# Causal mask added by VectorE on its way out of the banks, and two instructions moved in linear attention, in a six-layer decoder kernel

## The reference, cut to what matters

```python
def _L0_attn_ref(x, ...):                       # 16 heads of 16 features
    ...
    q = jnp.concatenate([q_c, _apply_rope(q_e, cos, sin)], axis=-1)
    k = jnp.concatenate([k_c, _apply_rope(k_e, cos, sin)], axis=-1)
    scores = jnp.einsum('bhqd,bhkd->bhqk', q, k) * scale
    causal = jnp.tril(jnp.ones((t, t), dtype=bool))
    scores = jnp.where(causal[None, None], scores, -jnp.inf)
    att = jax.nn.softmax(scores, axis=-1)
    y = jnp.einsum('bhqk,bhkd->bhqd', att, v)
    y = y.transpose(0, 2, 1, 3).reshape(b, t, c)
    return y @ Wc

def _L1_attn_ref(x, Wq, bq, Wk, bk, Wv, bv, Wo, bo):   # linear attention, 16 heads
    ...
    sink_incoming = 1.0 / jnp.einsum('nhld,nhd->nhl', q + EPS, k.sum(axis=2) + EPS)
    source_outgoing = 1.0 / jnp.einsum('nhld,nhd->nhl', k + EPS, q.sum(axis=2) + EPS)
    conserved_sink = jnp.einsum('nhld,nhd->nhl', q + EPS, (k * source_outgoing[..., None]).sum(axis=2) + EPS)
    conserved_source = jnp.einsum('nhld,nhd->nhl', k + EPS, (q * sink_incoming[..., None]).sum(axis=2) + EPS)
    conserved_source = jnp.clip(conserved_source, -1.0, 1.0)
    sink_allocation = jax.nn.sigmoid(conserved_sink * (float(l) / float(s)))
    source_competition = jax.nn.softmax(conserved_source, axis=-1) * float(s)
    kv = jnp.einsum('nhld,nhlm->nhdm', k, v * source_competition[..., None])
    out = jnp.einsum('nhld,nhdm->nhlm', q * sink_incoming[..., None], kv)
    out = out * sink_allocation[..., None]
    out = out.transpose(0, 2, 1, 3).reshape(b, l, D_MODEL)
    return out @ Wo.T + bo
```

## Time and profile before

| | |
|---|---|
| median of three runs | 2525.32 us (2520.55 to 2530.87) |
| the profiled execution, its own time | 2539.31 us |
| its span, first to last instruction | 2537.5 us, 58466 instructions |
| matmuls in flight on TensorE | 2118.6 us, 83% of the span |
| VectorE, ScalarE, GpSimd busy | 1530.8, 950.6, 928.1 us |
| self-attention | 0 to about 398 us |
| linear attention | about 1258 to about 1560 us |
| mean granted clock of TensorE | 0.887 |

### The profile page before, as it was taken

One profiled execution on the slowest core, in us unless ns is written; L12 is line 12 of the kernel. 1 busy time (PEld: TensorE's weight loads), 2 busy tenths in 40 slices (PEclk: granted clock), 3 DMA queues, 4 the chain that ended last, 5 costly groups with the idle time before them and its releaser, 6 DMA issues. The chain is left out here.

```text
span 2537.5 us, 58466 instructions
## 1 busy us (share of the span) xinstructions
PE 2118.6 (83%) x20310; PEld 1583.7 (62%) x20310; DVE 1530.8 (60%) x3550; ACT 950.6 (37%) x1881; POOL 928.1 (37%) x913
## 2 busy tenths in 40 slices
PE   6999997999776664788489996999999999996575
PEld 4666665777676554566388884666666666664233
DVE  1444443555454546233255455799999999984898
ACT  1444442333210110233134342344444444442897
POOL 0111111111134555223355431455555555553343
PEclk9999998999887786899789897899999999997555
DMA  6000003555311110877233311011110101000111
GB/s 208 30 29 29 29 25 130 207 205 212 133 48 35 34 33 23 259 222 221 73 100 90 98 44 46 21 32 31 32 32 23 32 31 32 30 13 9 52 58 46
DMA packets 157643, 192.74 MB, mean 76 GB/s; under 512 B 28517, under 2 KB 141160, under 8 KB 157559
## 3 DMA queue, kind: packets, MB, share of 16 engines
q1 hardware_dynamic: 147287, 189.03, 23.7%
q0 software_dynamic: 10272, 2.62, 0.5%
HBM read 140.74 MB, written 77.51 MB: 86 GB/s over the span
## 5 line engine op out<-in xcount | busy, mean ns | idle before, releaser
L2757 ACT ACTIVATE xa_prob<-xa_A 121x1600 f32<-121x1600 f32 x96 | 144.5, 1505 | 304.1 <-PE xa_A L2636 304.1
L2828 POOL TENSOR_TENSOR xa_prob<-xa_prob,xa_exp_bias 121x1600 f32<-121x1600 f32 x64 | 228.7, 3573 | 41.0 <-ACT xa_prob L2757 40.9
L2929 DVE TENSOR_REDUCE xa_kq<-xa_A 100x4 f32<-100x1444 f32 x128 | 211.6, 1653 | 21.3 <-PE xa_A L2609 21.1
L1409 POOL DMA_INDIRECT slot_rows<-rt_x_again,rt_slot_u x150 | 152.6, 1017 | 166.0 <-DVE rt_x_again L1527 103.5
L2909 DVE TENSOR_SCALAR xa_rows_n<-xa_rows_t,xa_mv,xa_rstd 121x256 f32<-121x256 f32 x128 | 142.4, 1172 | 1.1 <-POOL xa_rstd L2845 1.1
L2636 PEld LDWEIGHTS xa_A<-xa_q2T,xa_kqT 17*121 17x121 f32 x3072 | 93.9, 185 | 56.5 <-DVE xa_kq L2929 35.9
L696 DVE TENSOR_REDUCE sa_kq<-sa_A 100x16 f32<-100x1600 f32 x32 | 58.4, 1826 | 106.1 <-PE sa_A L457 106.1
L2609 PE MATMUL xa_A<-xa_kqT 16*100 16x361 f32 x1024 | 112.9, 510 | 9.9 <-ACT xa_prob L2757 6.8
L2636 PE MATMUL xa_A<-xa_q2T,xa_kqT 17*121 17x100 f32 x3072 | 109.3, 280 | 13.8 <-DVE xa_kq L2929 13.2
L1655 POOL DMA_INDIRECT contrib<-ex_y,ex_place_u x64 | 62.3, 973 | 158.5 <-ACT ex_y L1707 140.4
L2850 POOL TENSOR_TENSOR xa_o_rstd<-xa_o_var,xa_power 100x1 f32<-100x1 f32 x32 | 17.9, 560 | 252.1 <-DVE xa_o_var L2969 252.1
(11 more groups left out here) (350 smaller groups left out, 5397.0 us busy)
## 6 DMA issues: line engine op xcount, KB each, us to landing
ex_w<-in_w13T SPq DMA_DIRECT2D x64, 352.0 KB
contrib<-xs_zero SPq DMA_DIRECT2D x30, 640.0 KB
la_rows<-contrib SPq DMA_DIRECT2D x16, 1200.0 KB
xs_ctxT<-in_ctxT SPq DMA_DIRECT2D x32, 512.0 KB
xa_rows_t<-in_ctx SPq DMA_DIRECT2D x96, 121.0 KB
ex_w<-in_w2T SPq DMA_DIRECT2D x64, 176.0 KB
slot_rows<-xs_zero SPq DMA_DIRECT2D x32, 272.0 KB
ex_x_t<-slot_rows SPq DMA_DIRECT2D x64, 136.0 KB, 2.2
```

Of the source, the lines that this page charges most:

```text
L1409: nc.gpsimd.indirect_dma_start(slot_rows, bass.IndirectOffsetOnAxis(slot_u[:, k, n:n + 1], 0), x_again[:, k, :], None, bounds_check=SLOTS ...
L2757: nc.scalar.activation(prob[:, n, :].rearrange("p (h a) -> p h a", h=HPG), A[:ROWS, :, 0:G * T], ACT.Exp, scale=EXP_SCALE).then_inc(exp_re ...
L2828: nc.gpsimd.tensor_tensor(chunk, chunk, exp_bias[:, n, :].unsqueeze(1).to_broadcast([ROWS, HEADS, T]), ALU.mult).then_inc(biased, 1)
L2929: nc.vector.tensor_reduce(kq[:T, k, NCH, 4 * j:4 * j + 4, DH:DH + 1].rearrange("p h o -> p (h o)"), A[:T, :, 0:src_len], axis=AXIS_X, op=A ...
```

## The change

1. Self-attention, `score`: the four mask products L452 are removed and the scores are written to the banks directly (`start=True`). VectorE adds the mask instead: a new step `mask` adds a table `later_keys` (100 x 100, 0 or -1e30, repeated over the 16 heads) to the scores and writes the sum to a new tile `masked` in memory, 1600 numbers per partition.
2. `maxima` reads `masked` instead of the banks, and stands behind `rope` instead of ahead of it. `score_turned` waits for the new semaphore `masked_ready` instead of `max_ready`. The second kind of scores keeps its mask products.
3. SyncE loads `later_keys`, one more transfer that all engines wait for at the start.
4. Linear attention: on TensorE each of the first three keys-values products of unit b-1 comes ahead of the denominators of its group instead of behind them.
5. Linear attention: on VectorE `keep` is called for unit b between `residual` and `clip`, where it was called for unit b-1 between `gain` and `invert`.

```diff
@@ self_attention @@
+        later_keys = s.sb("later_keys", [T, T])
+        masked = s.sb("masked", [T, HPG, G * T])
-        W_ALL = 16 * 18
+        W_ALL = 16 * 19
                 sp.dma_start(causalf[:], w["causal"]).then_inc(w_in, 16)
+                sp.dma_start(later_keys[:], w["later_keys"]).then_inc(w_in, 16)
@@ TensorE, score @@
-                    for h in range(HPG):
-                        nc.tensor.matmul(A[:T, h, 0:G * T].rearrange("p (j t) -> p j t", t=T), causal[:],
-                                         identb[:].unsqueeze(1).to_broadcast([T, G, T]), start=True, stop=False, skip_group_check=True)
                     for j in range(G):
                         for h in range(HPG):
                             part = slice(32 * h, 32 * h + DH)
                             last = nc.tensor.matmul(A[:T, h, j * T:(j + 1) * T], kqT[part, k, j, T:2 * T], kqT[part, k, j, 0:T],
-                                                    start=False, stop=True, skip_group_check=True)
+                                                    start=True, stop=True)
@@ TensorE, score_turned @@
-                        pe.wait_ge(max_ready, at(later(b, 1), 1, 1))
+                        pe.wait_ge(masked_ready, at(later(b, 1), 1, 1))
@@ VectorE @@
+                def mask(b):
+                    dve.wait_ge(scored, at(b, 1, 1))
+                    dve.wait_ge(max_ready, at(later(b, -1), 1, 1))
+                    nc.vector.tensor_tensor(masked[:].rearrange("p h (j t) -> p h j t", t=T), A[:T, :, 0:G * T].rearrange("p h (j t) -> p h j t", t=T),
+                                            later_keys[:].unsqueeze(1).unsqueeze(1).to_broadcast([T, HPG, G, T]), ALU.add).then_inc(masked_ready, 1)
+
                 def maxima(b):
                     k = b[1] % 2
-                    dve.wait_ge(scored, at(b, 1, 1))
+                    dve.wait_ge(masked_ready, at(b, 1, 1))
                     dve.wait_ge(q2_turned, at(later(b, -2), 1, 1))
                     nc.vector.tensor_reduce(kq[:, k, 1, :, DH:DH + 1].rearrange("p (j h) o -> p j (h o)", j=G),
-                                            A[:T, :, 0:G * T].rearrange("p h (j t) -> p j h t", t=T),
+                                            masked[:].rearrange("p h (j t) -> p j h t", t=T),
                                             axis=AXIS_X, op=ALU.max).then_inc(max_ready, 1)
@@ VectorE, body @@
                     if has(1):
-                        maxima(later(b, 1))
+                        mask(later(b, 1))
                     if has(2):
                         rope(later(b, 2))
+                    if has(1):
+                        maxima(later(b, 1))
@@ linear_attention, TensorE, body @@
                     for n in range(4):
+                        if prev and n < 3:
+                            keys_values(later(b, -1), n)
                         if now:
                             denominators(b, KC * n)
-                        if prev and n >= 1:
-                            keys_values(later(b, -1), n - 1)
@@ linear_attention, VectorE, body @@
                     if has(-1):
                         gain(later(b, -1))
-                        keep(later(b, -1))
...
                     if has(-2):
                         residual(later(b, -2))
                     if has(0):
+                        keep(b)
                         clip(b)
@@ constants @@
+    c["later_keys"] = np.where(t[None, :] <= t[:, None], 0, NEG).astype(np.float32)
```

More of the change, by code:

```diff
@@ L327, in self_attention @@
         kq_turned, kqT_ready = s.sem("kq_turned"), s.sem("kqT_ready")
-        scored, max_ready = s.sem("scored"), s.sem("max_ready")
+        scored, masked_ready, max_ready = s.sem("scored"), s.sem("masked_ready"), s.sem("max_ready")
         q2_turned, q2_ready = s.sem("q2_turned"), s.sem("q2_ready")
@@ L676, in _ @@
                 nc.vector.memset(kq[:, :, 0, :, DH:DH + 1], -1.0).then_inc(cleared, 1)
-                for sem, per in ((roped, 1), (max_ready, 1), (rec_ready, 1), (y_ready, 1), (r_ready, 1), (o_stats_ready, 1), (o_mv_ready, 1),
+                for sem, per in ((roped, 1), (masked_ready, 1), (max_ready, 1), (rec_ready, 1), (y_ready, 1), (r_ready, 1), (o_stats_ready, 1), (o_mv_ready, 1),
                                  (o_var_ready, 1), (out_ready, 1)):
```

## The result

The changed kernel took 2503.3 us (median of 4 runs, 2496.9 to 2509.4) beside 2528.1 us for the kernel before (4 runs, 2520.6 to 2539.1): ratio 0.9889, 95% interval 0.9855 to 0.9922. That is 24.8 us less; the forecast was 27.4 less and 2498 us. The profiled execution took 2500.7 us, its span is 2498.9 us.

A forecast was written before the change was run, and what follows sets the result against it. TensorE's order was taken to bound self-attention, two touching loops linear attention. Mask products -27.3, load +0.4 and linear attention -0.5 sum to -27.4 us: median 2498, 8 in 10 for 2486 to 2511.

The forecast's parts named there:

- Mask products removed, 27.3 us: Self-attention, TensorE: dropping L452 saves 0.81 us in 30 batches and 1.50 in the first two; bounds 18 to 27.
- The mask takes 1.82 us and costs nothing: Self-attention, VectorE: the new addition takes 1.82 us where the maxima stood, so TensorE meets the same handover 0.81 earlier.
- no row has 1600 numbers with two operands: Claim that the earlier trace lacks the mask's size, so 1.82 us was priced from rows of 512 and 256 numbers.
- the first rival: Self-attention: mask addition slower than its row at other sizes; at 2.66 us it takes 27 us back; chance 0.05.
- Maxima behind the rotation, nothing; 1.8 a batch without that cover: Self-attention, VectorE: the moved 1.83 us reduction costs nothing, its reader coming 3 us later; uncovered, 1.8 us a batch.
- One more load, 0.4: Start, SP: the extra load delays TensorE's start by 0.38 us, once; bounds 0 and 2.
- Linear attention, -0.5: Linear attention: nine held periods 0.2 us slower, five 0.45 faster, sum -0.5 us; bounds -6 and +20.
- come 0.5 later: Linear attention, held period: GpSimd's next two additions, 1.27 us each, come 0.5 us later, to 13.4.
- What the profile after was to show: Signs: no L452, 9.8 us periods, 1.82 us addition, barrier near 371, L2255 mean 1.5 to 3, linear periods 15.6 to 15.9.
- Slower mask: Rival, self-attention: the mask addition is slower than priced; at 2.66 us the time is about 2525, no change; chance 0.05.
- GpSimd keeps winning: Rival, linear attention: held L2255 gets its turn only after L1929 and L1930; 20 us, time about 2518; chance 0.07.
- The clock: Rival, self-attention: TensorE's clock falls, 3.1 us per slow period; nine cancel the saving, twenty give 2560; chance 0.06.

The follow-up runs named there:

- e2: The kernel before with only the linear-attention part of the change, self-attention as before: 2388.3 us, ratio 0.9987.
- e7: The kernel before with only the new order of keys-values products and denominators in linear attention: 2545.1 us, one run.
- e8: The kernel before with only the bias addition of linear attention moved to its new place: 2536.4 us, one run.
- e9: The changed kernel with the inverse of linear attention's sums written back to its bank, so L2338 has one operand in memory: 2498.5 us, ratio 0.9865.
- e1: The kernel before with only the self-attention part of the change, linear attention as before: 2364.6 us, ratio 0.9890.
- e4: The changed kernel with the mask addition done twice in a row, masked_ready on the second: 2442.9 us, one run.
- e5: The changed kernel with the maxima called ahead of the rotation again, directly behind the mask addition: 2397.7 us, one run.
- e10: e9 and, in self-attention, TensorE multiplies the values of the block before ahead of turning the queries: 2479.7 us, ratio 0.9818 to the kernel before.

## Why the prediction was right, point by point

**Mask products removed, 27.3 us.** Right where it counts, in the steady periods; that the table's 27.2 meets it to 0.1 us is luck. From the first scores (49.94) to the last (378.35) it was 328.4 us, after (48.02 to 347.91) 299.9. In the 29 later periods the saving is 0.85 each against 0.81 taken: the 0.30 us of wait before the scores' weight load, which could have stayed, is 0.15 now. The start gave 1.9 us and the next two periods 3.9 (forecast 3.0 for the two masks at the lower level and 0.8 for the third): in the changed kernel L469 in the second period takes 0.54 us, where it took 0.90 at that place before, so TensorE's clock had risen a period earlier. That isn't the change's doing: in e2, e7 and e8, with self-attention as before, L469 takes 0.54 there too and the first two periods are 19.7 us together, not 23.5. Against that stands a loss after the last scores: from there to the next layer 26.1 us for 22.8. Most of it is the clock, at its lower level for some matmuls of the last period, seen where L486 takes 1.67 us. The table by stretches and the timeline of after, and the timeline of e2, which has self-attention as before:

```profile
90.00:350.00 260.00, 246.44 (x3554) 175.33 (x3554) 175.14 (x322) 122.15 (x243) 41.55 (x81) 1.00 0.11 31
350.00:370.00 20.00, 15.95 (x178) 11.30 (x178) 10.57 (x31) 5.70 (x9) 1.85 (x4) 0.83 0.10 27
```
```profile
350.92 0.85 PE L481 MATMUL sa_A<-sa_causal,sa_identb 100*100 100x400 bf16 x4 [1.72 <-DVE sa_masked L695]
351.69 1.67 PE L486 MATMUL sa_A<-sa_q2T,sa_kqT 17*100 17x100 f32 x32
```
```profile
378.12 1.67 PE L486 MATMUL sa_A<-sa_q2T,sa_kqT 17*100 17x100 f32 x32
```

L481 starts 3.01 us after the scores in both kernels (350.92 - 347.91, and 381.36 - 378.35 before), so the handover at the end costs nothing new. The slow L486 is there in two of the four executions with self-attention as before (e2, e8) and in all six with it changed, in e9 in part; so it doesn't need the change, and whether the change makes it likelier stays open. -1.9 at the start, -3.9 in two periods, -24.6 in 29 and +3.3 at the end make the -27.2 of the table. Between e2 and e1, on one chip and both with the slow end, the same four are -0.8, -2.0, -24.6 and +0.4, together -26.9: the 29 periods are the same, the rest is how each execution began and ended.

**The mask takes 1.82 us and costs nothing.** Right in size (1.825) and in place; e4 shows how near the edge that is. But a sentence of its working was wrong: "no row has 1600 numbers with two operands". The profile of before has one, VectorE's share of the bias in the last layer but one, which I had overlooked. In the groups by line of the kernel before:

```profile
L2936 DVE TENSOR_TENSOR xa_prob<-xa_prob,xa_exp_bias 121x1600 f32<-121x1600 f32 x32 | 57.9, 1810 | 1.9 <-ACT xa_prob L2757 1.9
```

It reads both operands from memory, not one from a bank, and gives 1.81. It would have narrowed the bounds of 1.77 to 2.66 and taken most of the chance of the first rival.

**Maxima behind the rotation, nothing; 1.8 a batch without that cover.** Right on the first: the division starts at once behind them (207.97) and the residual L720 has only its ordinary gap. On the second e5 gives 1.2 a batch (36.6 us over the stage), so some 0.6 of the 1.8 us was room that ScalarE's L581 and L587 had.

**One more load, 0.4.** Not seen. The new load is now the one that TensorE's first product waits for, until 17.14 us, where before it waited for `causalf` until 16.92. But over the executions that start is at 16.9 to 17.3 with self-attention as before and at 16.8 to 17.6 with it changed: a term of 0.4 can't be told from that spread. Nor can the 0.42 us by which the first scores come ahead of the place of the first mask product.

**Linear attention, -0.5.** Right in being near nothing (298.3 to 297.9 us, and e2's median 1.5 us less); two of its terms were mis-sized and cancel in part. Held periods were to be 0.2 us longer and are 0.09 shorter (15.43 for 15.52); free periods were to be 0.45 shorter and are 0.30. Counted from the first denominator, step by step against what was forecast: residual ends at 8.05 (8.1); L1931 ends at 10.15 (10.35); bias addition 10.70 (10.9); clip starts 10.82 (10.9); GpSimd's additions end at 13.06 (13.4); L2338 is done at 13.11 (13.45); the sums start at 13.75 (14.2); next denominators 15.37 (15.8). The step that failed is "come 0.5 later": L1937 lasts 1.60 where it takes 1.27 alone, 0.33 longer and not 0.5 (the 0.5 is how far another pair of the earlier trace rows stretched, L1933 behind L2337, and was taken over whole), and GpSimd had started 0.2 earlier. Nine times 0.29 us less than forecast is 2.6 us, five free periods 0.15 less each 0.75 the other way.

**What the profile after was to show.** Seen: no mask products, 9.7 us from scores to scores (9.8), the addition of 1.82 just ahead of L481's load, the barrier at 374 (near 371; the forecast took 27 from 398, and the stage before ended at 401.2), a mean of 2.1 us for the bias addition (1.5 to 3), L2338 longer, 15.13 us at the end. Not seen: full-clock periods of 15.6 to 15.9, but for one of 15.62.

**The rivals.** *Slower mask*: refuted, 1825 ns in all 32. *GpSimd keeps winning*: refuted, the bias addition ends 0.55 us behind L1931 and ahead of L1937, in a gap of 0.08 us. *The clock*: not in the steady periods of this kernel, where it is 1.00; falls in periods of this stage are in e4.

**The time.** 2503.3 is 5 above the forecast and in its range. Three comparisons, one of them without the linear part (e1), give 24.8, 25.2 and 24.6 us less; the traces of the stage give 27.2, 26.9 and, over all ten executions, 26.4. The intervals of the ratios, some 8 us either way, hold them all.

## What to carry to other kernels

Before moving work from a full engine to one with room, find the handover between them and ask if the new work ends no later than the old did; here it took the place of an equal reduction, and the reduction was put where something else was waited for. Where VectorE's instruction has both inputs in memory and GpSimd is in the middle of one that reads memory, it stood until GpSimd's was over: count it as the remaining time of GpSimd's plus its own less a little (0.14 us here), or give one of its inputs a bank. Read the whole list of groups for an instruction of the shape you are about to price, not only the stage that changes.

## What the runs showed of the hardware

- **A held instruction ends a little sooner behind its release than it takes alone.** The bias addition takes 0.69 us alone (L2255 before, mean 687 ns), and 0.55 from the end of L1931 to its own end; L1937, 1.27 alone, was done 1.13 us behind the end of the bias addition (1453.80 to 1454.93). L2338 takes 0.19 alone and ended 0.05 behind the end of L1938 (1456.16 to 1456.21). The wait hides some 0.14 us of each.
- **Regular waits went with a lower clock in one kernel and not in another.** The granted clock was 0.91 over 310 us in e4, where TensorE waited 1.7 us for VectorE in each period; it was 1.00 over 290 us in e5, where it waited 0.9 to 1.0 us before L521 and 0.4 to 0.5 before L469 in each, and 1.00 from 90 to 350 us in the changed kernel. What sets them apart no run here shows. In linear attention it fell in one to four of the 14 periods of most executions, in ten of e7's and in none of e10's, at places that differ between kernels and runs; why, no run here shows.
- **Chips differ by 6% on this program and not in these periods.** The kernel before took 2389.8 us on one chip and 2535.2 on another. The first layer ends at 372.4 in e1 and at 374.0 in the changed kernel; by the start of linear attention e1 is 142 us ahead (1078.1 against 1220.2), and by the end 132. So all of the difference arises in the layers between, and there in the two stretches of GpSimd's indirect transfers: from the first gather L1417 to the last it is 198.2 us in e1 and 297.3 after, from the first L1663 to the last 151.9 and 192.6. GpSimd's idle time before the gathers is 67.3 us in e1 and 167.1 after; the cause stays open.
